# First distance bias: from ahead of the attention tiles into them, every second part by ScalarE and GpSimd

## The chip, the cores and the metric

The kernel runs on one core of a Trainium2 chip. The time is device microseconds of one launch. The core has TensorE (PE), VectorE (DVE), ScalarE (ACT), GpSimd (POOL) and SyncE (SP, which issues DMAs here). Each engine runs its own instructions in the order of the program and waits on semaphores for the others.

## The reference, cut to what matters

Four layers of cross-attention and feed-forward run over x (2 x 1024 tokens of 256). Only two things matter here. The first cross-attention adds no learned bias, only a mask:

```
logits = einsum('btnh,bfnh->bnft', k, q) + bias
weights = softmax(logits);  ctx = einsum('bnft,btnh->bfnh', weights, v)
```

The second cross-attention is a decoder of four layers, and each of these adds a bias made from a distance for each query and key (1024 x 77 for each of 2 batches), by a small net of 32 hidden units:

```
hbias = relu(dist[..., None] @ Wth + bth)     # 32 values for each distance
qs_bias = (hbias @ Wto + bto)[..., 0]
```

So the bias is bto plus mask plus 32 parts, and part j is Wto[j] * relu(Wth[j] * dist + bth[j]). The bias of the decoder's first layer needs nothing that the first attention computes. It is made during it.

## The kernel before

Tokens are handled in NT = 16 tiles of 128. A row of scores is 16 heads x 77 keys = 1232 wide. The first attention is stage n = 0 of `act_wide`, `dve_wide` and `pe_wide`. Ahead of its tiles the keys are folded into the query weights (L513, copied at L596 and L657) and the values multiplied by the output weights (`values`, ten times: PE L490, ACT copy L576). Between these PE makes six small products (L335) that DVE copies (L340). DVE also takes the statistics of x (L3892, L225), GpSimd makes the inverse root (L240 to L268), and DVE normalises the first two tiles (L278).

Then for each tile t:

- PE: scores of tile t+1 (L478), turns the normalised rows of tile t+2 (`turn_tile`, L407), turns the weights of tile t (L448, waits for DVE's `weights_made`), weighs the values (L456).
- DVE: adds the mask (L736), maximum (L708), shift (L710), then `after_shift()` with what is given to go between, then the sum (L713, waits for ACT's exponential), reciprocal (L715), weights (L717), and the residual of tile t-1 (L725, L727).
- ACT: normalises tile t+2 (L671), exponential of tile t (L581), `keep_tile(t + 2)` (L571, waits for PE's turned rows), three copies of the turned weights (L631), then `after(t)`.

The word hinge in the code is one part j of the bias. `act_first_hinge` (L1407) makes the relu into one of two buffers, `first_hinge[:, j % 2]`, and waits until part j-2 has been added, since it reuses that buffer. `dve_first_hinge` (L1421) multiplies by `wto` and adds to `first_bias` in one instruction, after the relu of part j and the addition of part j-1. The last part is written to `flat_bias`, the bias buffer of the tiles, free once the tiles' masks have been added.

ACT makes 16 relus ahead of the tiles and one at the end of each tile. DVE adds 15 parts ahead of the tiles, one in `after_shift()` of each of the 16 tiles, and the last one behind them (`first_event`). So the part that DVE adds in tile t is 15+t, and its relu was made in tile t-1 or earlier.

GpSimd, during the tiles, builds the six weight matrices of the quantised feed-forward (`pool_dequantise`, L1391, L1393, L1396, once DMAs have brought their scales) and an inverse root for the first six tiles, and is otherwise idle. `EARLY` is 3 pairs of tiles; `w_made` counts the matrices.

Of the kernel before, what the change touches and what calls it, by code (L numbers as in the profile page):

```python
# [11 lines left out]
ACT = mybir.ActivationFunctionType  # L12
# [6 lines left out]
NT = B * TB  # L19
# [5 lines left out]
NTE = HE // P  # L25
# [14 lines left out]
HINGES = 32  # L40
# [25 lines left out]
def build(nc, ctx, a, out):  # L66
# [496 lines left out]
    def act_wide(act, n, clears, late, tail, between, after):  # L563

        g0 = NT * n

        def keep_tile(t):
            act.wait_ge(turned, g0 + t + 1)
            if t >= 2:
                act.wait_ge(scored, g0 + t - 1)  # L570
            act.copy(xnTt[:, t % 2, :, :].rearrange("p k c -> p (k c)"), xt_bank(t)).then_inc(xt_kept, 1)  # L571

        def values(v):
            bt, c = v // (CH // 2), 2 * (v % (CH // 2))
# [24 lines left out]
        if late:  # L599
            for v in range(VT_USES):  # L600
                values(v)
                if between:
                    between(v)
            keep_tile(0)
            keep_tile(1)
            if between:
                between("rows kept")
        else:
            keep_tile(0)
            keep_tile(1)  # L610
            for v in range(3):
                values(v)
            power(0)
            for v in range(3, VT_USES):
                values(v)
        for t in range(NT):
            base = t % 2 * 3 * BANK
            if n == 0 and t + 2 < NT:
                act_normed(act, n, t + 2)
            if t or late:  # L620
                power(t)
            if t + 2 < NT:
                keep_tile(t + 2)
            if t == NT - 1 and tail:
                tail()
            if t >= 2:
                act.wait_ge(weighed, g0 + t - 1)
            for i, chunks in enumerate(WIDE_GROUPS):
                b0, m = chunks[0], len(chunks)
                act.wait_ge(p_turned, 3 * (g0 + t) + i + 1)  # L630
                act.copy(wide_probT[:, t % 2, b0:b0 + m, :].rearrange("p c n -> p (c n)"),  # L631
                         flat[:, base + b0 * P:base + (b0 + m) * P]).then_inc(p_kept, 1)
            if after:
                after(t)
# [595 lines left out]
    EARLY = 3  # L1230
# [134 lines left out]
                    vs()  # L1365

    def pool_quantised(pool):
        pool_root(pool, 1e-5, 0, 2 * EARLY)
        pool.wait_ge(rows_of_bias_landed, 16)
        for i in range(EVENTS + 1):  # L1370
            if i < EVENTS:
                pool.wait_ge(h_turned, i + 1)
                pool.tensor_tensor(pair_of(inner, i), pair_of(inner, i),
                                   brow[:, 2 * (i // PAIRS) + 1:2 * (i // PAIRS) + 2, :].to_broadcast([P, 2, D]), ALU.add).then_inc(h_biased, 1)
            if i >= 1:
                t = 2 * ((i - 1) % PAIRS)
                pool_root(pool, 1e-5, t, t + 2)
            if i == 1:
                pool_root(pool, 1e-5, 2 * EARLY, NT - 2)
                pool_root(pool, 1e-5, NT - 2, NT)  # L1380

    def pool_dequantise(pool):
        pool.wait_ge(quants_landed, 16 * 11)
        pool.wait_ge(products_kept, NL + KD)
        for j in range(NL):
            at = slice(j * KD * D, (j + 1) * KD * D)
            if j:
                pool.wait_ge(w_made, j)  # L1390
            pool.tensor_scalar(dequant, quants[:, at], 1.0 / 7.5, -1.0, ALU.mult, ALU.add).then_inc(pool_step, 1)  # L1391
            pool.wait_ge(pool_step, gs())
            pool.tensor_tensor(dequant, dequant, scales[:, KD * j:KD * j + KD, :].rearrange("p n o -> p (n o)"),  # L1393
                               ALU.mult).then_inc(pool_step, 1)
            pool.wait_ge(pool_step, gs())
            pool.tensor_tensor(WT[:, j, :, :].rearrange("p k o -> p (k o)"), WT[:, j, :, :].rearrange("p k o -> p (k o)"), dequant,  # L1396
                               ALU.add).then_inc(w_made, 1)

    def act_first_hinge(act, j):
        if j == 0:
            act.wait_ge(distance_landed, 64)
            act.wait_ge(fside_landed, 16)
        if j >= 2:
            act.wait_ge(hinge_added, j - 1)
        act.activation(first_hinge[:, j % 2, :], flat_side, ACT.Relu, scale=wth[:, j:j + 1], bias=bth[:, j:j + 1]).then_inc(hinge_made, 1)  # L1407

    def dve_first_hinge(dve, j):
        if j == 0:  # L1410
            dve.wait_ge(distance_landed, 64)
            dve.wait_ge(mask_landed, 16)
            by_tile = first_bias.rearrange("p (t s) -> p t s", s=S2)
            for bt in range(B):
                dve.tensor_scalar(by_tile[:, bt * TB:(bt + 1) * TB, :], mask[:, bt, :].unsqueeze(1).to_broadcast([P, TB, S2]),
                                  bto[:, 0:1], None, ALU.add).then_inc(dve_step, 1)
                dve.wait_ge(dve_step, vs())
        else:
            dve.wait_ge(hinge_added, j)
        dve.wait_ge(hinge_made, j + 1)  # L1420
        dve.scalar_tensor_tensor(first_bias if j < HINGES - 1 else flat_bias, first_hinge[:, j % 2, :], wto[:, j:j + 1], first_bias,  # L1421
                                 ALU.mult, ALU.add).then_inc(hinge_added, 1)


# [19 lines left out]
    class Hinges:  # L1444
# [15 lines left out]
        def dve(self, dve):  # L1460
# [6 lines left out]
                                      bto[:, 0:1], None, ALU.add).then_inc(dve_step, 1)  # L1467
                    dve.wait_ge(dve_step, vs())
            elif j < HINGES:
                dve.wait_ge(hinge_made, base + j + 1)  # L1470
                if j:
                    dve.wait_ge(hinge_added, base + j)
                dve.scalar_tensor_tensor(flat_bias, hinge[:, j % 2, :], wto[:, j:j + 1], flat_bias,  # L1473
                                         ALU.mult, ALU.add).then_inc(hinge_added, 1)
# [2391 lines left out]
    def act_program(act):  # L3866
# [1 line left out]
        hinges = iter(range(HINGES))  # L3868

        def between(done):  # L3870
            for _ in range({"values expanded": 2, "keys folded": 3, "rows kept": 4, 0: 0, VT_USES - 2: 0, VT_USES - 1: 0}.get(done, 1)):
                act_first_hinge(act, next(hinges))

        act_wide(act, 0, 1, True, lambda: act_quantised(act, 0, 2), between, lambda t: [act_first_hinge(act, j) for j in [next(hinges, None)] if j is not None])
        act.wait_ge(quants_landed, 16 * 11)
        act_quantised(act, 2, EVENTS + LAG_G)
        act_decoder(act)
# [4 lines left out]

    def dve_program(dve):
        dve_setup(dve)
        hinges = iter(range(HINGES))

        dve_wide_values(dve, 0, 1, lambda: dve_first_hinge(dve, next(hinges)))
        for _ in range(2):
            dve_first_hinge(dve, next(hinges))
        dve.wait_ge(x_landed, 48)  # L3890
        for t in range(NT):
            dve.bn_stats(bn6[:, t, :], x[:, t, :]).then_inc(dve_step, 1)  # L3892
            vs()
        dve_aggregate(dve)
        for j in range(2, NL):
            dve_first_hinge(dve, next(hinges))
            dve_first_hinge(dve, next(hinges))
            dve_lora(dve, j)
        dve_first_hinge(dve, next(hinges))
        dve.wait_ge(tanh_made, 1)  # L3900
        dve_root(dve)
        for t in range(2):
            dve_normed(dve, 0, x, t)
        for _ in range(3):
            dve_first_hinge(dve, next(hinges))

        def one_more(t):
            for j in [next(hinges, None)]:
# [10 lines left out]
        def first_event():  # L3919
            dve.wait_ge(rows_of_bias_landed, 16)  # L3920
            dve_quantised(dve, 0, 1)
            dve_aggregate(dve, 2 * EARLY, NT - 2)
            for j in hinges:
                dve_first_hinge(dve, j)

        dve_wide(dve, 0, x, tanh_g[:, 0:1], one_more, first_event)
        dve_aggregate(dve, NT - 2, NT)
# [7 lines left out]
    def pool_program(pool):  # L3935
# [3 lines left out]
        pool_centers(pool, 0, NT)  # L3939
        pool.wait_ge(products_kept, NL + KD)  # L3940
        pool_clear_pads(pool)
        pool_dequantise(pool)
        pool_quantised(pool)
        pool_clear_expanded(pool)
        pool.wait_ge(h_product, EVENTS)
# [71 lines left out]
```

## Time and profile before

| | us |
|---|---|
| median of 3 runs | 3079.68 (3072.37 to 3088.09) |
| the profiled execution | 3078.32 |
| its span | 3077.1 |
| before the first tile's mask addition | 65.0 |
| the 16 tiles of the first attention | about 65 to 224 |
| PE, DVE, ACT, POOL busy over the span | 96%, 68%, 40%, 28% |
| mean granted clock of TensorE | 0.989 |

Times in the rows are from the start of the span. A row of the timeline is one or several like instructions in order of time: start, how long, engine, line, what is written and read, how many, and in brackets how long the engine was idle before and which engine released it. The overall shares say little of this change, which lies in the first 230 us. There the stretches and the timelines tell.

### The profile page before, as it was taken

The page shows a single profiled execution, that of the slowest core. Times are in us where ns is not written, and L with a number is a line of the kernel's source. Part 1 is how long each engine was busy: PE and PEld are TensorE (multiplying, and loading weights), DVE is VectorE, ACT ScalarE, POOL GpSimd, SP SyncE. Part 2 cuts the span into 40 slices and gives each one's busy share as a digit, 9 for nine tenths or more (in the row PEclk, how much of TensorE's full clock was granted, in tenths as well). Part 3 has the DMA queues.
Part 4 walks back from the last instruction along what each step waited for, and adds up shares of the span by engine and source line. Part 5 has one row for each costly group of instructions (what it writes and reads, how often), then busy time and mean ns, then how long its engine had stood idle before and what let it go on. Part 6 is the DMA issues. An engine that isn't in the chain of part 4 may idle for free.

```text
span 3077.1 us, 44737 instructions
## 1 busy us (share of the span) xinstructions
PE 2951.9 (96%) x16886; PEld 2141.5 (70%) x16886; DVE 2089.9 (68%) x3855; ACT 1227.2 (40%) x2303; POOL 876.2 (28%) x1321
## 2 busy tenths in 40 slices
PE   7999899999999999999999999999999989998999
PEld 5778677667766776677689989866667754556565
DVE  6996689568856885687378898784317877774222
ACT  5443323553355335433233323451224556564232
POOL 2307300100110010001156565551342332111565
PEclk8999999999999999999999999999999999999999
DMA  7000100010002000200022222003361011113744
GB/s 186 28 1 1 58 1 1 14 44 28 1 14 72 1 1 14 71 1 1 1 85 82 89 82 83 30 1 110 130 246 56 4 46 53 33 47 131 212 85 98
DMA packets 106353, 172.32 MB, mean 56 GB/s; under 512 B 28842, under 2 KB 78925, under 8 KB 101405
## 3 DMA queue, kind: packets, MB, share of 16 engines
q1 hardware_dynamic: 87516, 98.10, 10.4%
q0 software_dynamic: 18624, 71.37, 7.6%
q8 instruction: 136, 2.23, 0.3%
q14 instruction: 77, 0.62, 0.1%
HBM read 193.86 MB, written 17.84 MB: 69 GB/s over the span
## 4 chain that ended last, share of the span: by engine, by line
PE 74%; DVE 15%; issue 4%; DMA 3%; ACT 3%; POOL 1%; SPq 0%; DVEq 0%; POOLq 0%; ACTq 0%
PE psum L456 8%; PE psum L478 8%; PE psum L1547 7%; PE psum L1559 7%; PE psum L2716 5%; PE psum L2028 5%; PE psum L1983 5%; PE psum L2737 3%; PE psum L1257 2%; PE psum L448 2%; PE psum L829 2%; PE psum L3368 2%; PE psum L2866 2%; DVE prep L1421 1%; PE psum L3388 1%
## 5 line engine op out<-in xcount | busy, mean ns | idle before, releaser
L456 PE MATMUL psum<-Vt,shared 128*128 128x256 f32 x1600 | 358.9, 379 | 0.2
L478 PE MATMUL psum<-Kt,xnTt 128*128 128x512 f32 (+1 forms) x960 | 348.6, 513 | 0.4 <-ACT xnTt L571 0.3
L456 PEld LDWEIGHTS psum<-Vt,shared 128*128 128x128 f32 x1600 | 297.7, 190 | 38.2 <-issue 1.0
L478 PEld LDWEIGHTS psum<-Kt,xnTt 128*128 128x128 f32 x960 | 181.0, 192 | 162.7 <-issue 159.1
L247 POOL TENSOR_SCALAR root_v<-meanvar 128x8 f32<-128x8 f32 (+3 forms) x19 | 8.6, 454 | 880.5 <-DVE meanvar L225 880.5
L1559 PEld LDWEIGHTS psum<-expert_w,prep 128*128 128x128 f32 x1024 | 194.6, 190 | 77.7 <-issue 57.4
L1559 PE MATMUL psum<-expert_w,prep 128*128 128x256 f32 x1024 | 240.8, 379 | 0.0
L1547 PE MATMUL psum<-weights,expert_w 128*128 128x512 f32 x512 | 240.3, 593 | 0.0
L1473 DVE SCALAR_TENSOR_TENSOR bias<-Kt,small,bias 128x1232 f32<-128x1232 f32 x96 | 149.2, 1554 | 129.3 <-ACT Kt L1457 128.4
L3657 DVE CUSTOM_DVE_ANT_0 psum<-psum,expert_w 128x128 f32<-128x128 f32 (+7 forms) x256 | 191.1, 777 | 65.9 <-PE psum L3368 61.9
L2823 DVE TENSOR_TENSOR prep<-psum,prep 128x512 f32<-128x512 f32 x62 | 42.9, 692 | 218.0 <-PE psum L2716 201.4
L3544 ACT ACTIVATE prep<-psum 128x512 f32<-128x512 f32 (+3 forms) x384 | 163.1, 504 | 63.6 <-PE psum L3391 61.5
L1602 ACT ACTIVATE prep<-psum,bias 128x512 f32<-128x512 f32 x128 | 87.9, 687 | 237.3 <-PE psum L1547 237.3
L581 ACT ACTIVATE shared<-shared 128x1232 f32<-128x1232 f32 x80 | 98.7, 1233 | 181.9 <-DVE shared L710 181.9
L713 DVE TENSOR_REDUCE row<-shared 128x16 f32<-128x1232 f32 x80 | 114.7, 1434 | 55.3 <-ACT shared L581 55.3
L571 ACT COPY xnTt<-psum 128x256 f32<-128x256 f32 x80 | 29.4, 372 | 298.9 <-PE psum L407 298.8
L1547 PEld LDWEIGHTS psum<-weights,expert_w 128*128 128x128 f32 x512 | 96.1, 190 | 69.1 <-issue 63.1
L736 DVE TENSOR_TENSOR shared<-psum,bias 128x1232 f32<-128x1232 f32 x80 | 115.0, 1438 | 36.5 <-PE psum L478 33.1
L1457 ACT ACTIVATE Kt<-fside,small 128x1232 f32<-128x1232 f32 x96 | 134.5, 1404 | 1.5 <-DVE bias L1473 1.5
L631 ACT COPY shared<-psum 128x512 f32<-128x512 f32 (+1 forms) x240 | 115.4, 517 | 39.7 <-PE psum L448 38.6
L3368 PE MATMUL psum<-weights 72*128 72x512 bf16 (+3 forms) x384 | 106.7, 333 | 19.7 <-DVE row L3657 18.0
L3388 PE MATMUL psum<-weights 75*128 75x512 bf16 (+3 forms) x384 | 113.0, 333 | 7.5 <-DVE Kt L3597 3.0
(529 smaller groups left out, 6546.5 us busy)
## 6 DMA issues: line engine op xcount, KB each, us to landing
weights<-in_L_ffn_w SPq DMA_DIRECT2D x32, 512.0 KB, 4.9
expert_w<-in_L_ffn_w SPq DMA_DIRECT2D x32, 512.0 KB, 4.8
expert_w<-in_L_xattn_Wf SPq DMA_DIRECT2D x16, 512.0 KB, 5.9
weights<-q_parts SPq DMA_DIRECT2D x31, 144.0 KB
weights<-k_parts SPq DMA_DIRECT2D x93, 48.0 KB
weights<-in_L_xattn_Wk SPq DMA_DIRECT2D x4, 1024.0 KB, 5.0
weights<-in_L_xattn_Wv SPq DMA_DIRECT2D x4, 1024.0 KB, 7.6
weights<-in_L_xattn_Wq SPq DMA_DIRECT2D x4, 1024.0 KB, 5.5
```

The lines of the kernel that those rows point to most:

```text
L456: ins = pe.matmul(o_bank(t), wide_probT[:, t % 2, c, :], Vt[:, t // TB, c, :], start=(c == 8), stop=(c == 7))
L478: ins = pe.matmul(flat[:, par * 3 * BANK + at:par * 3 * BANK + at + cols], xnTt[:, par, k, :], Kt[:, t // TB, k, src:src + cols], start=(k ...
L1473: dve.scalar_tensor_tensor(flat_bias, hinge[:, j % 2, :], wto[:, j:j + 1], flat_bias, ALU.mult, ALU.add).then_inc(hinge_added, 1)
L1547: ins = pe.matmul(bank, slot(s)[0][:, k, f * P:(f + 1) * P], xnT_of(g)[:, k, :], start=(k == 0), stop=(k == KD - 1))
L1559: ins = pe.matmul(y[:, t * D:(t + 1) * D], hidden[:, n % 4, t * P:(t + 1) * P], slot(s)[2][:, f, :], start=(n % GROUP_STEPS == 0 and t % 2 ...
L1983: return pe.matmul(product_of(i), lhs, rhs, start=start, stop=stop, skip_group_check=True)
L2028: ins = pe.matmul(acc_of(i)[:, t * P:(t + 1) * P], lhs[:, t * P:(t + 1) * P], rhs, start=(begin and start and t == 0), stop=end, skip_grou ...
L2716: ins = pe.matmul(psum[:, 2 * (c % 2) + n, :], rows_xT[:, c % 2, k, :], w[:, at:at + F], start=(k == 0), stop=(k == KD - 1))
L3368: ins = pe.matmul(flat[:, base + at:base + at + w], heads[0:STACK, 0, s, t * P:(t + 1) * P], heads[0:STACK, 1, s, at:at + w], start=True, ...
L3388: ins = pe.matmul(psum[:, bank, 0:w], heads[:, 1, s, j * P:(j + 1) * P], heads[:, 0, s, at:at + w], start=True, stop=True)
L3544: act.activation(expT[:, h % 2, to:to + w], psum[:, ring_bank(("piece", h, i)), 0:w], ACT.Exp, scale=float(HD3) ** -0.5).then_inc(exp_made, 1)
L3657: dve.tensor_tensor_reduce(flat[:, base:base + cols], flat[:, base:base + cols], later[:, S - cols:S], 1.0, -3.0e38, ALU.add, ALU.max, max ...
```

## The change

- The order of ACT: four relus ahead of the tiles (two behind the values' expansion, two behind the folded keys), none between the copies of the values. The other 28 are made two in each of tiles 0 to 13. For this `act_wide` calls `after(t)` a second time, behind `keep_tile(t + 2)` and ahead of the three copies.
- Odd parts from 5 on (14 parts) are not DVE's. ACT multiplies the relu by `wto` in place (a second instruction, which waits for the first) and GpSimd adds it to `first_bias`.
- DVE adds 18 parts: 0 to 3 ahead of the tiles, and 4, 6, ... 30 in `after_shift()` of tiles 0 to 13.
- GpSimd adds part 5+2j ahead of building matrix j, for six matrices, then two more, then the inverse root for the first six tiles, then six more; the last waits for all shifts and writes `flat_bias`.
- `hinge_made` now counts twice for an odd part, so the wait of the later layers has a constant more.

```diff
@@ act_wide, in the loop over tiles
             if t + 2 < NT:
                 keep_tile(t + 2)
+            if after:
+                after(t)
@@ pool_dequantise
         for j in range(NL):
+            pool_first_hinge(pool, next(hinges))
@@
+    HINGES_AHEAD = 4
+    def on_pool(j):
+        return j > HINGES_AHEAD and j % 2 == 1
+    def first_made_by(j):
+        return j + 1 + sum(map(on_pool, range(j + 1)))
+    def pool_first_hinge(pool, j):
+        pool.wait_ge(hinge_added, j)
+        if j == HINGES - 1:
+            pool.wait_ge(shifted, NT)
+        pool.wait_ge(hinge_made, first_made_by(j))
+        pool.tensor_tensor(first_bias if j < HINGES - 1 else flat_bias, first_hinge[:, 1, :], first_bias, ALU.add).then_inc(hinge_added, 1)
@@ act_first_hinge
-        act.activation(first_hinge[:, j % 2, :], flat_side, ACT.Relu, scale=wth[:, j:j + 1], bias=bth[:, j:j + 1]).then_inc(hinge_made, 1)
+        ins = act.activation(first_hinge[:, j % 2, :], flat_side, ACT.Relu, scale=wth[:, j:j + 1], bias=bth[:, j:j + 1])
+        if on_pool(j):
+            ins.then_inc(hinge_made, 1)
+            act.wait_ge(hinge_made, first_made_by(j) - 1)
+            ins = act.mul(first_hinge[:, 1, :], first_hinge[:, 1, :], wto[:, j:j + 1])
+        ins.then_inc(hinge_made, 1)
@@ dve_first_hinge
-        dve.wait_ge(hinge_made, j + 1)
+        dve.wait_ge(hinge_made, first_made_by(j))
@@ act_program
-            for _ in range({"values expanded": 2, "keys folded": 3, "rows kept": 4, 0: 0, VT_USES - 2: 0, VT_USES - 1: 0}.get(done, 1)):
+            for _ in range({"values expanded": 2, "keys folded": 2}.get(done, 0)):
@@ pool_program
-        pool_dequantise(pool)
+        hinges = iter(j for j in range(HINGES) if on_pool(j))
+        pool_dequantise(pool, hinges)
+        for _ in range(NTE - NL):
+            pool_first_hinge(pool, next(hinges))
+        pool_root(pool, 1e-5, 0, 2 * EARLY)
+        for j in hinges:
+            pool_first_hinge(pool, j)
```

Two places in the programs of the engines. First ACT, one tile near the start of the tiles, from the normalisation of tile t+2 (`xn`) to that of the next. `inner` is the hinge buffer. Before:

```order
L671 ACTIVATE xn<-x,center,rstd 128x256 [waits turned,factors_made]
L581 ACTIVATE shared<-shared 128x8x154 [waits shifted]
L571 COPY xnTt<-psum 128x256 [waits scored,turned]
L631 COPY shared<-psum 128x256 [waits p_turned]
L631 COPY shared<-psum 128x512 [waits p_turned] x2
L1407 ACTIVATE inner<-fside,small 128x1232 [waits hinge_added]
```

And now, the same place:

```order
L673 ACTIVATE xn<-x,center,rstd 128x256 [waits turned,factors_made]
L581 ACTIVATE shared<-shared 128x8x154 [waits shifted]
L571 COPY xnTt<-psum 128x256 [waits scored,turned]
L1426 ACTIVATE inner<-fside,small 128x1232 [waits hinge_added]
L633 COPY shared<-psum 128x256 [waits p_turned]
L633 COPY shared<-psum 128x512 [waits p_turned] x2
L1426 ACTIVATE inner<-fside,small 128x1232 [waits hinge_added]
L1430 ACTIVATE inner<-inner,small 128x1232 [waits hinge_made]
```

One relu has come between the exponential with the copy of the turned rows and the three copies. A multiplication has come behind the other relu. Second DVE, ahead of the tiles, from the statistics of x to the mask addition of tile 0. Before:

```order
L225 BN_AGGR meanvar<-bn6 128x2 x15
L1421 SCALAR_TENSOR_TENSOR prep<-inner,small,prep 128x1232 [waits hinge_made,hinge_added] x2
L340 COPY expert_w<-psum 128x512 [waits products_set_up]
...
L1421 SCALAR_TENSOR_TENSOR prep<-inner,small,prep 128x1232 [waits hinge_made,hinge_added]
L278 TENSOR_SCALAR xn<-x,meanvar,rstd 128x256 [waits root_made,tanh_made]
L278 TENSOR_SCALAR xn<-x,meanvar,rstd 128x256
L1421 SCALAR_TENSOR_TENSOR prep<-inner,small,prep 128x1232 [waits hinge_made,hinge_added] x3
L736 TENSOR_TENSOR shared<-psum,bias 128x8x154 [waits scored]
```

And now:

```order
L225 BN_AGGR meanvar<-bn6 128x2 x15
L340 COPY expert_w<-psum 128x512 [waits products_set_up] x4
L1445 SCALAR_TENSOR_TENSOR prep<-inner,small,prep 128x1232 [waits hinge_made,hinge_added]
L278 TENSOR_SCALAR xn<-x,meanvar,rstd 128x256 [waits root_made,tanh_made]
L278 TENSOR_SCALAR xn<-x,meanvar,rstd 128x256
L1445 SCALAR_TENSOR_TENSOR prep<-inner,small,prep 128x1232 [waits hinge_made,hinge_added]
L738 TENSOR_TENSOR shared<-psum,bias 128x8x154 [waits scored]
```

Of the twelve additions between the statistics and tile 0 two are left. Inside a tile DVE's own order is as it was: mask, maximum, shift, one part of the bias, sum.

## Rows read from the trace of the kernel before

**Rows 1.** Stretches: span, PE, PEld, DVE, ACT, POOL busy, clock, DMA, GB/s.

```profile
73.93:204.13 130.20, 128.02 (x572) 94.82 (x572) 127.99 (x128) 62.11 (x91) 26.90 (x22) 1.00 0.07 25
```

**Rows 2.** Waits from 66 to 222: who for whom, total us, times, longest.

```profile
ACT xnTt L571 <- PE psum L407: 49.9, 13, 4.4
```

**Rows 3.** Timeline of DVE: weights of tiles 0 and 13, and of a tile between.

```profile
72.46 1.46 DVE L717 TENSOR_TENSOR shared<-shared,row 128x1232 f32<-128x1232 f32 x1
...
139.12 1.49 DVE L1421 SCALAR_TENSOR_TENSOR prep<-inner,small,prep 128x1232 f32<-128x1232 f32 x1
...
142.28 1.44 DVE L717 TENSOR_TENSOR shared<-shared,row 128x1232 f32<-128x1232 f32 x1
...
202.69 1.44 DVE L717 TENSOR_TENSOR shared<-shared,row 128x1232 f32<-128x1232 f32 x1
```

**Rows 4.** Timeline of PE, one tile: turned weights, and the next scores.

```profile
84.06 1.31 PE L448 MATMUL psum<-ident,shared 128*128 128x128 f32 x10
...
89.53 4.30 PE L478 MATMUL psum<-Kt,xnTt 128*128 128x512 f32 x12
```

**Rows 5.** Timeline of ACT, the same tile.

```profile
84.54 1.51 ACT L631 COPY shared<-psum 128x256 f32<-128x256 f32 x3
85.93 1.43 ACT L1407 ACTIVATE inner<-fside,small 128x1232 f32<-128x1232 f32 x1
...
94.08 0.37 ACT L571 COPY xnTt<-psum 128x256 f32<-128x256 f32 x1 [2.96 <-PE psum L407]
```

**Rows 6.** Timeline, the last part: relu of ACT, then DVE, which waited.

```profile
225.94 1.43 ACT L1407 ACTIVATE inner<-fside,small 128x1232 f32<-128x1232 f32 x1
...
227.47 1.50 DVE L1421 SCALAR_TENSOR_TENSOR bias<-inner,small,prep 128x1232 f32<-128x1232 f32 x1 [0.41 <-ACT inner L1407]
```

**Rows 7.** Timeline, tile 0: DVE's mask addition, ACT's exponential and copy.

```profile
65.00 1.44 DVE L736 TENSOR_TENSOR shared<-psum,bias 128x1232 f32<-128x1232 f32 x1
...
69.42 1.23 ACT L581 ACTIVATE shared<-shared 128x1232 f32<-128x1232 f32 x1 [3.95 <-DVE shared L710]
70.56 0.35 ACT L571 COPY xnTt<-psum 128x256 f32<-128x256 f32 x1
```

**Rows 8.** Timeline ahead of the tiles: PE's values and products, GpSimd's root.

```profile
37.47 2.83 PE L490 MATMUL psum<-weights,prep 128*32 128x256 f32 x32 [2.53 <-ACT Vt L576]
40.23 2.07 PE L335 MATMUL psum<-shared 32*128 32x256 f32 x4
...
49.85 1.93 PE L490 MATMUL psum<-weights,prep 128*32 128x256 f32 x32
51.72 1.13 PE L335 MATMUL psum<-shared 32*128 32x256 f32 x4
...
49.15 1.34 POOL L268 TENSOR_TENSOR rstd<-rstd,root_w 128x16 f32<-128x16 f32 x1
```

**Rows 9.** Stretches: granted clock of TensorE ahead of the tiles.

```profile
46.00:48.00 2.00, 2.00 (x24) 0.67 (x20) 1.96 (x2) 2.00 (x3) 1.92 (x2) 0.50 0.00 0
```

**Rows 10.** Timeline of PE: the scores of tiles 0 and 1, in two attentions.

```profile
57.98 0.67 PE L407 MATMUL psum<-ident,xn 128*128 128x128 f32 x4 [2.69 <-DVE xn L278]
58.95 10.15 PE L478 MATMUL psum<-Kt,xnTt 128*128 128x512 f32 x24 [0.29 <-ACT xnTt L571]
...
378.02 11.04 PE L478 MATMUL psum<-Kt,xnTt 128*128 128x512 f32 x24
```

**Rows 11.** GpSimd: a wide addition by form, and one line with min/median/max in ns.

```profile
L1727 POOL TENSOR_TENSOR inner<-inner,small 128x1024 f32<-128x1024 f32 x16 | 41.6, 2603 | 186.3 <-DVE prep L278 173.8 <-DVE Kt L278 12.5
...
L1393 POOL TENSOR_TENSOR prep<-prep x6: 1267/1278/2335, 71.4 to 95.9; 128x512 f32<-128x512 f32 x6
```

**Rows 12.** Timeline: DVE beside GpSimd, DVE's extra rows, GpSimd at the end.

```profile
78.36 2.52 DVE L1421 SCALAR_TENSOR_TENSOR prep<-inner,small,prep 128x1232 f32<-128x1232 f32 x1
...
200.29 0.73 DVE L278 TENSOR_SCALAR inner<-x,meanvar,rstd 128x256 f32<-128x256 f32 x2
...
226.62 0.23 POOL L245 TENSOR_SCALAR root_v<-meanvar 128x2 f32<-128x2 f32 x1 [3.91 <-DVE meanvar L225]
```

More of the change, by code:

```diff
@@ L1367, in pool_quantised @@
     def pool_quantised(pool):
-        pool_root(pool, 1e-5, 0, 2 * EARLY)
         pool.wait_ge(rows_of_bias_landed, 16)
@@ L1380, in pool_quantised, with pool_dequantise @@
                 pool_root(pool, 1e-5, NT - 2, NT)
-    def pool_dequantise(pool):
+    def pool_dequantise(pool, hinges):
         pool.wait_ge(quants_landed, 16 * 11)
@@ L1419, in dve_first_hinge @@
             dve.wait_ge(hinge_added, j)
-        dve.wait_ge(hinge_made, j + 1)
-        dve.scalar_tensor_tensor(first_bias if j < HINGES - 1 else flat_bias, first_hinge[:, j % 2, :], wto[:, j:j + 1], first_bias,
+        dve.wait_ge(hinge_made, first_made_by(j))
+        dve.scalar_tensor_tensor(first_bias, first_hinge[:, j % 2, :], wto[:, j:j + 1], first_bias,
                                  ALU.mult, ALU.add).then_inc(hinge_added, 1)
@@ L1469, in dve @@
             elif j < HINGES:
-                dve.wait_ge(hinge_made, base + j + 1)
+                dve.wait_ge(hinge_made, base + j + 1 + first_made_by(HINGES - 1) - HINGES)
                 if j:
@@ L3870, in between, with beside @@
         def between(done):
-            for _ in range({"values expanded": 2, "keys folded": 3, "rows kept": 4, 0: 0, VT_USES - 2: 0, VT_USES - 1: 0}.get(done, 1)):
+            for _ in range({"values expanded": 2, "keys folded": 2}.get(done, 0)):
                 act_first_hinge(act, next(hinges))
-        act_wide(act, 0, 1, True, lambda: act_quantised(act, 0, 2), between, lambda t: [act_first_hinge(act, j) for j in [next(hinges, None)] if j is not None])
+        def beside(t):
+            for j in [next(hinges, None)]:
+                if j is not None:
+                    act_first_hinge(act, j)
+        act_wide(act, 0, 1, True, lambda: act_quantised(act, 0, 2), between, beside)
         act.wait_ge(quants_landed, 16 * 11)
@@ L3884, in dve_program @@
         dve_setup(dve)
-        hinges = iter(range(HINGES))
+        hinges = iter(j for j in range(HINGES) if not on_pool(j))
         dve_wide_values(dve, 0, 1, lambda: dve_first_hinge(dve, next(hinges)))
-        for _ in range(2):
-            dve_first_hinge(dve, next(hinges))
+        dve_first_hinge(dve, next(hinges))
         dve.wait_ge(x_landed, 48)
@@ L3895, in dve_program @@
         for j in range(2, NL):
-            dve_first_hinge(dve, next(hinges))
-            dve_first_hinge(dve, next(hinges))
             dve_lora(dve, j)
@@ L3903, in dve_program @@
             dve_normed(dve, 0, x, t)
-        for _ in range(3):
-            dve_first_hinge(dve, next(hinges))
+        dve_first_hinge(dve, next(hinges))
         def one_more(t):
@@ L3922, in first_event @@
             dve_aggregate(dve, 2 * EARLY, NT - 2)
-            for j in hinges:
-                dve_first_hinge(dve, j)
+            dve.wait_ge(hinge_added, HINGES)
         dve_wide(dve, 0, x, tanh_g[:, 0:1], one_more, first_event)
```

## The prediction

> **What bounds the kernel now.** I read the stretch of the first attention first, since the change lies in it. Between the weights of tile 0 and of tile 13 both PE (128.02 of 130.20) and DVE (127.99) are full [rows 1]. 13 tiles take 202.69 - 72.46 = 130.2 us, 10.0 each [rows 3]. ACT is half idle and GpSimd four fifths. So ACT's and GpSimd's busy time is free here, but not their place in the chain of waits. DVE's addition of one part (1.49 us) also is no loss in a tile: it stands between the shift and the sum, and the sum needs ACT's exponential (1.23) anyway [rows 3, 7].
>
> Next I read what ACT waits for inside a tile. Its copy of the turned rows, `keep_tile(t + 2)`, waited 49.9 us for PE in 13 of the tiles, 3.8 each [rows 2]. In PE's program the turn of tile t+2 stands behind the weighing of tile t-1 and the scores of tile t+1. One tile shows it: PE starts to turn the weights at 84.06, starts the next scores at 89.53 for 4.30, and only then turns the rows; ACT's copy runs from 94.08 to 94.45 [rows 4, 5]. From the moment the weights of a tile are there to the end of that copy is thus 94.45 - 84.06 = 10.39 us. Today nothing of DVE hangs on it within the tile.
>
> **The change, part by part.** *The new wait.* DVE adds part 4+2t in tile t, between shift and sum, and ACT makes the relu of just that part in the same tile, behind the exponential and behind `keep_tile(t + 2)`. Before, DVE's part was 15+t and its relu a tile old. Now DVE stands at the part until PE has turned the rows, ACT has copied them and made the relu. Queued behind it on DVE are the sum, the reciprocal and the weights, and PE waits for the weights to turn them, with the weighing and the next scores behind. That closes a loop through three engines, from weights to weights:
>
> - DVE to PE, a hand-over: 0.10 (the one from ACT to DVE is 227.47 - 227.37 = 0.10) [rows 6];
> - PE turns weights, weighs, scores, turns rows, ACT copies: 10.39 [rows 4, 5];
> - the relu: 1.43 less the 0.12 by which it starts ahead of the copy's end (85.93 against 86.05): 1.31 [rows 5];
> - ACT to DVE: 0.10 [rows 6];
> - DVE from part to the end of the weights: 142.28 + 1.44 - 139.12 = 4.60 [rows 3].
>
> The sum is 16.5 us. The steps between tiles 0 and 13 are 13, so 13 x 16.5 = 214.6 in place of 130.2: **+84.4**. The mask addition, maximum and shift of the next tile, ACT's exponential and the residual fit beside PE's 10.39 and cost nothing; that cover stays, since PE gets no less work. In tiles 11 to 13 two rows normalised between part and sum (0.65 each) were hidden partly and now lie in the loop: **+2.0** [rows 12]. For its 14 parts the turned rows exist in all tiles, 0 to 13 (t+2 below 16).
>
> *Tile 0.* From the mask addition to the exponential's start are 4.42 us, the copy ends at 5.91 [rows 7], then relu 1.31, 0.10 and DVE's 4.60: 11.9. Before, 65.00 to 73.92 = 8.9 [rows 3, 7]. **+3.0.**
>
> *The clock of TensorE.* In the loop PE works 10.4 us and stands about 6. The clock granted ahead of the tiles is 0.50, 1.2 GHz, in places [rows 9]. The scores of tiles 0 and 1 took 10.15 us with 2.69 us of idle time ahead of PE's turn before them, and 11.04 in the next attention; two tiles' scores at full clock take 2 x 4.30 = 8.60 [rows 4, 10]. So a stand that lets the clock fall costs 1.55 to 2.44 us. The lower bound is 0 (the clock holds), the upper 2.44. I take 1.55, the row with the shorter stand: 13 x 1.55 = **+20.2**.
>
> *Tiles 14 and 15* have no part. In tile 14 PE still has its weighing and scores of 9.77 (84.06 to 93.83) [rows 4] with the 1.55, 11.3 against about 9.7 now: **+1.7** (0 to 2).
>
> *Ahead of the tiles.* DVE loses 11 additions, 16.5 us of it, ACT 12 relus. That does not all come back. What is late next is either GpSimd's root, ready at 50.49 and 1.5 earlier if the statistics start one part earlier, which gives 49.0, rows normalised and turned until 50.7, scores of tile 0 (half of 10.15) until 55.8, and 9.2 us gained [rows 8, 10]. Or it is PE's values: from 37.47 less one relu, 36.0, eight values (four pairs of 1.93) and three products of 1.13 are 11.1 us at full clock; at the lower clock a product takes 2.07, 1.83 times as long, and all 20.3 [rows 8]. Bounds for the tiles' start are then 9.2 and 2.6 earlier. The clock was still low at 46 to 48 [rows 9]. With 12 us at that pace, 12 / 1.83 = 6.6 of the 11.1 are done at 48 and the other 4.5 at 52.5; 0.97 for turning and copying and 5.1 for the scores make 58.5 instead of 65.0: **-6.5**.
>
> *ACT's and GpSimd's new work.* The second relu and the multiplication (not in the trace; taken as another 1.4, bounds 1.2 and 1.5 from the exponential and the relu) begin behind the three copies, which end 1.99 us into the loop [rows 4, 5], so they end near 4.8. GpSimd's addition of 1232 elements: 2.60 x 1232/1024 = 3.1 us, up to 1.83 times that, 5.7, by the spread of its 512-wide one [rows 11]. It ends at 8 to 10.5, and DVE asks for it at 11.9. Its three instructions for a matrix follow and end before the next. So none of it is on the path: 0. It can lengthen a DVE instruction that runs beside it: 2.52 against 1.49 once [rows 12]. In the loop DVE stands while GpSimd adds, so I take 0, with 14 x 1.03 = 14.4 as the upper end. In the Trainium skill, "SBUF — State Buffer", section "Who interferes with whom", a DVE instruction with two SBUF inputs and a GpSimd instruction that reads SBUF block each other for the whole instruction, the later one waiting. By that rule the sum could be up to 14 x 3.1 = 43 us more, an estimate; the 2.52 agrees that there is such a cost, and the rule speaks against the change wherever DVE does not stand anyway.
>
> *The end.* DVE's last part (1.50) goes, but it stood ahead of a residual that waited for PE: 0. GpSimd's last part (3.1) fits the 3.91 us that it was idle there [rows 12]: 0, up to 2.
>
> Sum: -6.5 + 3.0 + 84.4 + 2.0 + 20.2 + 1.7 = +104.8. On the profiled execution's own 3078.3 this gives **3183.1**; it lies 1.4 below the median of the runs shown, which is less than they spread. The later layers keep their order.
>
> **The rivals.** (a) *The relu is early enough*, and the kernel gets faster: if DVE found the relu ready within about 1.3 us of its shift (the length of the exponential), the tiles would stay at 10.0 and only the start count: 3078.3 - 6.5 = 3072. For it speaks ACT's idle half; against it that ACT runs in order and the relu is third behind exponential and copy. 3 in 100.
>
> (b) *The wait without the loop*: if PE's turned rows were there when the exponential ends, as in tile 0, the stand would be 4.42 to 5.91 and the relu, 2.9 us a tile. 13 x 2.9 = 38, less 130.2 - 13 x 9.7 = 4 of old stalls, + 3.0 - 6.5 + 2.0: near 3111. Against it are the 3.8 us that ACT waits for PE in each tile [rows 2], with PE already full. 5 in 100.
>
> (c) *TensorE stays at 1.2 GHz* through the tiles: PE's 10 us of each tile get 1.83 times as long, +8.3, so 13 x 8.3 = 108 in place of 20.2: 3270. Against it are the scores of tiles 0 and 1, which took only 1.55 us more than at full clock, so that it came back within them [rows 10]. 4 in 100.
>
> **How the numbers follow.** The loop as worked out has 88 in 100. Its ends: -9.2 + 3.0 + 84.4 + 2.0 + 0 + 0 = +80 (3158) with the clock held, and -2.6 + 3.0 + 84.4 + 2.0 + 31.7 + 14.4 + 2 + 2 = +137 (3215). The range 3157 to 3213 leaves out the rivals and the far end. A measurement tells about 0.5%, 15 us. Faster by more: 3 in 100 at most, half of (a) being within 0.5%; I give 0.02, the same 0.02, slower 0.96.
>
> **What would show it.** In the trace after: DVE's part in a tile (L1445) with an idle time before it of some 6 us, released by ACT's relu; ACT's copy L571 waiting for PE, and the relu right behind it; PE's turned weights (L448) waiting for DVE in tiles 1 to 13; tiles 16 to 19 us apart, then under 12; the granted clock at 0.50 for a part of each tile; the first mask addition near 58.5. GpSimd's additions end before DVE asks. If the relu is ahead of the copy in time, or the tiles are under 13 us apart, the loop is wrong. If they are over 20, the clock or GpSimd was priced too low.

## The result, and the profile after

The changed kernel takes **3183.4 us** (median of 4 executions, 3180.6 to 3190.3) against 3078.5 (4 executions, 3072.4 to 3088.1): ratio **1.034** [1.032, 1.036], 104.9 us slower. The profiled execution is the slowest of the four, 3190.25 with a span of 3189.0, 111.9 above the span of before; terms read from it are some us larger than those of the median. The change acts up to the start of the scores of the second attention. Up to there the profiled execution takes 486.11 against 378.02 [rows 10], 108.1 more; the other 3.8 lie in the later layers, which the change leaves alone: from there to the end the twelve profiled executions of this document take between 2691 and 2707.

Stretches of the kernel after. The columns are those of [rows 1]; the first two lie ahead of the tiles, the next around the work of PE in tile 1, the last is nearly the whole of the tiles.

```profile
40.00:44.00 4.00, 4.00 (x57) 2.09 (x49) 2.53 (x14) 1.75 (x3) 3.16 (x2) 1.00 0.00 2
44.00:48.00 4.00, 3.26 (x39) 1.83 (x40) 2.94 (x5) 1.76 (x3) 1.56 (x9) 1.00 0.10 25
...
65.00:82.00 17.00, 12.74 (x44) 9.55 (x44) 6.52 (x5) 7.47 (x9) 5.92 (x4) 0.80 0.46 153
...
60.00:320.00 260.00, 168.21 (x605) 127.21 (x606) 138.12 (x139) 102.70 (x124) 58.58 (x37) 0.78 0.06 20
```

Where PE and DVE were both busy for 128 of 130 us [rows 1], they are now busy for 168 and 138 of 260, at a granted clock of 0.78. Nobody is the bound; everybody waits. Who waits for whom from 60 to 320 us:

```profile
POOL prep L1418 <- ACT inner L1430: 186.9, 13, 24.9
DVE prep L1445 <- ACT inner L1426: 120.3, 14, 10.4
PE psum L448 <- DVE shared L719: 92.0, 14, 7.1
...
ACT xnTt L571 <- PE psum L407: 64.5, 13, 5.6
```

Read the last three upwards: ACT's copy waits for PE's turned rows (49.9 before [rows 2]), DVE's part waits for the relu behind that copy, PE's turn of the weights waits for DVE. That is a ring. The first line is the longest and costs nothing, as run 3 shows: GpSimd is early. One turn of the ring, from the weights of tile 0 to those of tile 1, in the timelines of DVE, PE and ACT (start, us, engine, line, operation, in brackets the idle time before it and who ended it):

```profile
53.01 1.44 DVE L738 TENSOR_TENSOR shared<-psum,bias 128x1232 f32<-128x1232 f32 x1 [3.79 <-PE psum L478]
...
63.51 1.44 DVE L719 TENSOR_TENSOR shared<-shared,row 128x1232 f32<-128x1232 f32 x1
...
79.66 1.50 DVE L1445 SCALAR_TENSOR_TENSOR prep<-inner,small,prep 128x1232 f32<-128x1232 f32 x1 [10.41 <-ACT inner L1426]
...
82.83 1.44 DVE L719 TENSOR_TENSOR shared<-shared,row 128x1232 f32<-128x1232 f32 x1
...
309.18 1.44 DVE L719 TENSOR_TENSOR shared<-shared,row 128x1232 f32<-128x1232 f32 x1
...
319.28 1.44 DVE L719 TENSOR_TENSOR shared<-shared,row 128x1232 f32<-128x1232 f32 x1
...
323.34 1.44 DVE L738 TENSOR_TENSOR shared<-psum,bias 128x1232 f32<-128x1232 f32 x1 [1.77 <-PE psum L478]
...
330.79 2.41 DVE L719 TENSOR_TENSOR shared<-shared,row 128x1232 f32<-128x1232 f32 x1
```

```profile
65.10 2.37 PE L448 MATMUL psum<-ident,shared 128*128 128x128 f32 x10 [5.31 <-DVE shared L719]
67.26 6.22 PE L456 MATMUL psum<-Vt,shared 128*128 128x256 f32 x20
73.32 4.30 PE L478 MATMUL psum<-Kt,xnTt 128*128 128x512 f32 x12
...
84.33 2.40 PE L448 MATMUL psum<-ident,shared 128*128 128x128 f32 x10 [6.49 <-DVE shared L719]
86.52 5.14 PE L456 MATMUL psum<-Vt,shared 128*128 128x256 f32 x20
91.50 4.30 PE L478 MATMUL psum<-Kt,xnTt 128*128 128x512 f32 x12
```

```profile
77.88 0.37 ACT L571 COPY xnTt<-psum 128x256 f32<-128x256 f32 x1 [5.51 <-PE psum L407]
78.14 1.41 ACT L1426 ACTIVATE inner<-fside,small 128x1232 f32<-128x1232 f32 x1
...
96.05 0.37 ACT L571 COPY xnTt<-psum 128x256 f32<-128x256 f32 x1 [4.42 <-PE psum L407]
```

The relu ends at 79.55 and DVE starts at 79.66, after 10.41 us of standing; from there to the end of its weights are 84.27 - 79.66 = 4.61. PE, having stood for 5.31 or 6.49 us, is granted the lower clock when it starts: turning (1.31 at full clock [rows 4]) takes 2.4. From weights to weights it is 82.83 - 63.51 = 19.3, then 18.2, and so on in turns; turning and weighing take 8.22 (65.10 to 73.32) in one tile and 7.17 (84.33 to 91.50) in the next, against 5.47 before [rows 4].

### The profile page after: what moved, and what is told of

The parts are those of the page before. It is cut to its first block, busy times and chain, and to the rows that moved or that the text cites. A ratio compares the mean times of both kernels' runs of the same rounds, so it can differ in the third digit from the quotient of the medians.

```text
span 3189.0 us, 44752 instructions
## 1 busy us (share of the span) xinstructions
PE 2988.3 (94%) x16886; PEld 2171.8 (68%) x16886; DVE 2069.6 (65%) x3841; ACT 1247.1 (39%) x2317; POOL 901.4 (28%) x1335
## 4 chain that ended last, share of the span: by engine, by line
PE 76%; DVE 11%; issue 4%; ACT 3%; DMA 3%; POOL 2%; SPq 0%; DVEq 0%; POOLq 0%; ACTq 0%
PE psum L456 11%; PE psum L478 10%; PE psum L1571 7%; PE psum L1583 6%; PE psum L2052 5%; PE psum L2007 5%; PE psum L2740 4%; PE psum L448 3%; PE psum L1259 2%; PE psum L3392 2%; PE psum L831 2%; PE psum L2761 2%; DMA out<-shared,prep 2%; PE psum L2890 2%; PE psum L3412 2%
## 5 line engine op out<-in xcount | busy, mean ns | idle before, releaser
L456 PE MATMUL psum<-Vt,shared 128*128 128x256 f32 x1600 | 376.3, 392 | 0.2
L456 PEld LDWEIGHTS psum<-Vt,shared 128*128 128x128 f32 x1600 | 311.6, 199 | 43.1 <-issue 1.0
L448 PE MATMUL psum<-ident,shared 128*128 128x128 f32 x800 | 116.6, 300 | 98.2 <-DVE shared L719 98.2
L448 PEld LDWEIGHTS psum<-ident,shared 128*128 128x128 f32 x800 | 101.9, 155 | 105.4 <-DVE shared L719 96.2
L633 ACT COPY shared<-psum 128x512 f32<-128x512 f32 (+1 forms) x240 | 116.7, 517 | 125.3 <-PE psum L448 124.8
```

What stands on the lines that cost most here:

```text
L448: ins = pe.transpose(flat[:, base + c * P:base + (c + 1) * P], rows[:, c * P:(c + 1) * P], ident[:, :])
L456: ins = pe.matmul(o_bank(t), wide_probT[:, t % 2, c, :], Vt[:, t // TB, c, :], start=(c == 8), stop=(c == 7))
```

## The experiments

Ten runs, each with its own median, and a ratio to the kernel before, run beside it on the same chip. Runs 1 to 4 shared a chip, so did 5 to 7, and 9 and 10; the kernel before had medians of 3082.8, 3079.8, 3076.9 (run 8) and 3078.0 there, so medians of different chips compare only to some 6 us. Where it matters, the start of the second attention's scores in the profiled execution is given too.

### 1. Two more relus ahead: is it the wait?

```diff
-            for _ in range({"values expanded": 2, "keys folded": 2}.get(done, 0)):
+            for _ in range({"values expanded": 2, "keys folded": 2, "rows kept": 2}.get(done, 0)):
```

> The changed kernel with parts 4 and 5 made by ScalarE ahead of the tiles (behind the copies of the first two turned tiles), so that in tile t it makes 6+2t and 7+2t and VectorE's part 4+2t is a tile old. Theory (VectorE stands for a relu behind the copy of the turned rows, and that closes the loop): the stands go, tiles fall from 18.9 us to about 10, and the earlier start (12 us by the trace) is kept: 3066 to 3076. Rival (two parts a tile are too much beside the attention, for ScalarE or for GpSimd and VectorE together): tiles stay above 15, 3140 or more.

**3085.3**, ratio 1.0005 [0.999, 1.002], 9 above the upper end. ACT is now a part ahead, and 98 of the 105 us are gone: the wait is the cause. But the kernel isn't faster than before, although its first mask addition starts 12 us earlier. Its timelines of DVE, ACT and PE, one tile:

```profile
106.13 1.73 DVE L719 TENSOR_TENSOR shared<-shared,row 128x1232 f32<-128x1232 f32 x1
...
108.45 1.42 ACT L1426 ACTIVATE inner<-fside,small 128x1232 f32<-128x1232 f32 x1
...
109.76 1.33 ACT L633 COPY shared<-psum 128x256 f32<-128x256 f32 x3
...
110.27 4.56 PE L456 MATMUL psum<-Vt,shared 128*128 128x256 f32 x20 [1.03 <-ACT shared L633]
...
117.17 1.44 DVE L719 TENSOR_TENSOR shared<-shared,row 128x1232 f32<-128x1232 f32 x1
```

The relu stands ahead of the three copies of the turned weights, so PE waits 1.03 us to weigh in nine of the tiles, 9.3 in all, and such a tile takes 11.04 (117.17 - 106.13) instead of 10. The 13 steps from tile 0 to 13 take 147.7 in place of 130.2, which is more than that. Most of the rest are instructions of DVE that run long beside GpSimd: in tile 11 the two normalised rows take 3.21, in place of 0.73 [rows 12], beside an addition of 2.90, and the tile takes 12.8. Together they more than eat the 12 us of the start: the second attention's scores start at 382.9 against 378.0.

### 2. The odd relu before the copy of the rows

```diff
+            if after:
+                after(t)
             if t + 2 < NT:
                 keep_tile(t + 2)
-            if after:
-                after(t)
```

> The changed kernel with the first relu of a tile ahead of the copy of the turned rows instead of behind it; all else is the same, and VectorE still waits for a relu of its own tile. Theory: the stand shrinks to exponential plus relu, 2.7 us, TensorE is out of the loop, tiles of 12.3 to 12.8 us: 13 x 6.2 = 81 less than the changed kernel, 3100 to 3106. Rival (any wait for a relu of the same tile costs it, the copy does not matter): above 3150.

**3115.7**, ratio 1.011 [1.007, 1.014], 10 above the upper end; the tiles take 12.5 to 14.3. The relu doesn't wait for the copy any more, but a smaller ring takes its place, which I had not seen. Waits, and the timelines of GpSimd and DVE in one tile:

```profile
DVE prep L1445 <- POOL prep L1418: 41.9, 13, 4.5
```

```profile
113.04 2.81 POOL L1418 TENSOR_TENSOR prep<-inner,prep 128x1232 f32<-128x1232 f32 x1 [7.18 <-ACT inner L1430]
...
115.92 1.81 DVE L1445 SCALAR_TENSOR_TENSOR prep<-inner,small,prep 128x1232 f32<-128x1232 f32 x1 [3.61 <-POOL prep L1418]
```

The odd part now is the late one: its relu and multiplication stand behind the three copies, GpSimd adds only then, and DVE must wait for that sum before it adds its own part.

### 3. GpSimd's addition and ACT's multiplication one element wide

```diff
-        pool.tensor_tensor(first_bias if j < HINGES - 1 else flat_bias, first_hinge[:, 1, :], first_bias, ALU.add).then_inc(hinge_added, 1)
+        pool.tensor_tensor((first_bias if j < HINGES - 1 else flat_bias)[:, 0:1], first_hinge[:, 1, 0:1], first_bias[:, 0:1], ALU.add).then_inc(hinge_added, 1)
...
-            ins = act.mul(first_hinge[:, 1, :], first_hinge[:, 1, :], wto[:, j:j + 1])
+            ins = act.mul(first_hinge[:, 1, 0:1], first_hinge[:, 1, 0:1], wto[:, j:j + 1])
```

> The changed kernel with GpSimd's additions and ScalarE's multiplications one element wide instead of 1232, so 14 of the 32 parts are not added; the waits are the same. Theory: neither is on the path of the loop, 3178 to 3186, tiles still 18 to 19 us. Rival (GpSimd's 2.8 us additions or ScalarE's multiplication pace the tiles, or block VectorE): 36 us less or more, under 3150.

**3186.9**, ratio 1.033 [1.030, 1.037]: no gain, though 14 of the 32 parts are left out; the second attention's scores start at 485.3 against 486.1. In the changed kernel the new work of GpSimd and of ACT's multiplication costs nothing.

### 4. TensorE kept at work while it would stand

```diff
+            if n == 0 and 1 <= t <= 13:
+                pe.wait_ge(shifted, g0 + t + 1)
+                pe_stay_at_work(pe, flat[:, t % 2 * 3 * BANK:t % 2 * 3 * BANK + P], 26)
             pe_turn_wide(pe, n, t)
```

> The changed kernel with 26 idle matmuls of 128 columns on TensorE in the stand of each tile 1 to 13 (about 6.2 us, ending about when the weights come), into a score bank that is free by then. Theory (part of the loop is the clock that falls during the stand): granted clock 1.00 through the tiles, tiles of 16.6 to 16.9 us, 13 x 2.2 = 29 less than the changed kernel, 3150 to 3158. Rival (the clock costs nothing, the loop is longer for another reason): the same as the changed kernel, 3180 to 3187.

**3156.6**, ratio 1.024 [1.020, 1.027], 26.8 below the changed kernel, 30.3 below run 3 on the same chip, and 28.5 to the start of the second attention's scores. The edit fills 13 of the 14 stands: the one before PE turns tile 0's weights stays, and so the step from tile 0 to 1 still takes 19.5. The granted clock from 64 to 285 us is 0.98, and the loop can be seen bare in PE's timeline:

```profile
100.94 1.31 PE L448 MATMUL psum<-ident,shared 128*128 128x128 f32 x10 [0.68 <-DVE shared L722]
102.09 4.48 PE L456 MATMUL psum<-Vt,shared 128*128 128x256 f32 x20
106.41 4.30 PE L478 MATMUL psum<-Kt,xnTt 128*128 128x512 f32 x12
110.54 0.38 PE L407 MATMUL psum<-ident,xn 128*128 128x128 f32 x2
110.76 5.97 PE L413 MATMUL psum<-ident 128*128 128x128 f32 x52
117.41 1.31 PE L448 MATMUL psum<-ident,shared 128*128 128x128 f32 x10 [0.68 <-DVE shared L722]
```

117.41 - 100.94 = 16.47 us. The sum of the five steps was 16.5. In tiles 11 to 13 a step takes 17.12, 3 x 0.65 = 2.0 more in all, as predicted for the two normalised rows.

### 5. Where do the 12 us at the start go?

As run 1, with the additions and multiplications of run 3.

> The kernel with two more parts ahead (tiles of 11.0 us in the middle, no faster than before) and GpSimd's additions and ScalarE's multiplications one element wide, so 14 of the 32 parts are not added. Theory (in that kernel VectorE waits some 1.3 us a tile for an exponential that ScalarE's two relus and multiplication push back; without the 1.3 us multiplication most of that goes): tiles near 10, 3066 to 3074, 11 to 19 less than that kernel. Rival (what is left there is TensorE's own pace): within 5 us of it, 3080 to 3086.

**3073.4**, ratio 0.998 [0.997, 0.9995]. That lies in the theory's range, but by luck: the tiles still take 11.04 in the middle where it had 10, and `PE psum L456 <- ACT shared L633` still adds up to 12.4 us in 12 tiles. So the 1.0 us a tile is the relu's place ahead of the copies, as said under 1, and neither the multiplication nor GpSimd. What these two cost comes on top: 12 us by the medians of two chips, 6.0 by the start of the second attention's scores (376.99 against 382.94), and tiles 11 and 12 are back at 11.0.

### 6 and 7. The odd part in ACT's wait, the even one behind the copies

Run 6 has the order of run 2 and one relu more ahead (`"rows kept": 1`), so that the part that ACT makes before the copy of the rows is the odd one, and the one behind the copies the even one of the next tile. Run 7 has GpSimd's addition one element wide besides.

> The changed kernel with one more part ahead (part 4) and the first of a tile's two parts ahead of the copy of the turned rows, so that the relu and multiplication for GpSimd (2.8 us) fall into ScalarE's wait of 3.8 us for TensorE, and the relu for VectorE's next tile behind the three copies. Theory: no stand of VectorE, exponential and copies on time, tiles of 9.7 to 10, the earlier start kept: 3065 to 3073, faster than before. Rival (GpSimd's additions beside VectorE's two-operand instructions cost what the start gives): 3076 to 3084, no difference from before.

> The kernel with the odd parts ahead of the copy, GpSimd's additions one element wide (14 parts not added); ScalarE as there. The difference is what GpSimd's 2.8 us additions cost VectorE. Theory: 1 to 10 us less than that kernel. Rival: 15 us less or more.

Run 6: **3074.3**, ratio 0.998 [0.997, 0.9995] (12 executions). Run 7: **3058.8**, ratio 0.9935 [0.992, 0.995]. The theory had 1 to 10 us for the difference, the rival 15 or more. It is 15.4 by the medians and 11.8 by the start of the second attention's scores (375.52 against 363.73); no run shows where the other 3.6 come from. Either way GpSimd's 14 additions do cost something once DVE has no idle time. In run 7 most tiles take 9.67, and DVE is full. In the profiled execution of run 6, the slowest of its twelve, GpSimd, DVE and PE in one tile:

```profile
106.46 2.78 POOL L1418 TENSOR_TENSOR prep<-inner,prep 128x1232 f32<-128x1232 f32 x1 [2.94 <-ACT inner L1430]
106.48 4.05 DVE L719 TENSOR_TENSOR shared<-shared,row 128x1232 f32<-128x1232 f32 x1
...
110.59 2.40 PE L448 MATMUL psum<-ident,shared 128*128 128x128 f32 x10 [4.08 <-DVE shared L719]
```

DVE's product, started 0.02 after GpSimd's addition, takes 4.05 instead of 1.44, 2.61 more, nearly the 2.78 of GpSimd; PE stands for it and starts at the lower clock. The Trainium skill, "SBUF — State Buffer", section "Who interferes with whom", says that a DVE instruction with two SBUF inputs and a GpSimd instruction that reads SBUF block each other for the whole instruction; by that rule, the trace agrees. Such tiles are those in which GpSimd also builds its matrices: the steps from tile 0 to 6 take 11.7 more than in run 7 (up to 12.3 each), and the nine after them 0.2 more, although eight of the 14 additions lie there. They fall beside other instructions of DVE, which keep their length; GpSimd, then DVE:

```profile
131.62 3.13 POOL L1418 TENSOR_TENSOR prep<-inner,prep 128x1232 f32<-128x1232 f32 x1 [5.46 <-ACT inner L1430]
...
131.99 0.48 DVE L727 SCALAR_TENSOR_TENSOR x<-psum,tanh_g,x 128x256 f32<-128x256 f32 x1
132.50 0.43 DVE L729 BATCH_NORM_STATS2 bn<-x 128x6 f32<-128x256 f32 x1
132.93 1.44 DVE L738 TENSOR_TENSOR shared<-psum,bias 128x1232 f32<-128x1232 f32 x1
134.41 1.44 DVE L710 TENSOR_REDUCE row<-shared 128x16 f32<-128x1232 f32 x1
```

### 8 to 10. Placing GpSimd's work

All three start from run 6. In run 8 DVE makes the odd parts 5 to 13 itself, so that GpSimd has its matrices alone. Run 9 is run 8 in which each matrix, and each addition of GpSimd, waits until DVE has written the tile's weights. Run 10 is run 6 with that wait for the additions only.

```diff
     def pool_dequantise(pool, hinges):
...
         for j in range(NL):
-            pool_first_hinge(pool, next(hinges))
+            pool.wait_ge(weights_made, j + 1)
...
     def on_pool(j):
-        return j > HINGES_AHEAD and j % 2 == 1
+        return j > 13 and j % 2 == 1
...
     def pool_first_hinge(pool, j):
...
+        pool.wait_ge(weights_made, (j - 3) // 2)
...
         def one_more(t):
...
                     dve_first_hinge(dve, j)
+                    if j % 2 == 1:
+                        dve_first_hinge(dve, next(hinges))
```

> As the odd part ahead of the copies, but VectorE makes the odd parts 5, 7, 9, 11 and 13 itself, one more addition in each of tiles 1 to 5, and GpSimd adds only 15, 17, ... 31 (from tile 5 on), so that it has nothing but its matrices in the tiles before. All is computed. Theory (of the 15.4 us that GpSimd's additions cost, all arise in the tiles in which it also makes matrices, since from tile 6 on the tiles of that run took 9.67 to 9.77): the tiles 1 to 5 take 9.67 + 1.45 = 11.1 each, the rest 9.7; the time is that with GpSimd's additions one element wide and five VectorE additions, 3058.8 + 5 x 1.45 = 3066, 3062 to 3071. Rival (each addition of GpSimd costs the same wherever it stands, 15.4 / 14 = 1.1): 3066 + 9 x 1.1 = 3076, 3073 to 3080, with tiles of 10.8 from the sixth on.

> As the run before it (VectorE makes the odd parts 5 to 13, GpSimd adds from 15 on), and each of GpSimd's six matrices, and each of its additions, waits until VectorE has finished the tile's last product (L719), so that what GpSimd does falls beside VectorE's residual, the mask addition out of PSUM and the maximum. All is computed. Theory (in the run before, the six matrices in one row from 61.9 to 90.9 beside L712, the additions and L719 cost 5.1 in tiles 1 and 2, and one addition beside L719 cost 2.4): the tiles 1 to 5 come to 11.2 each, tile 5 loses the stretched L719; 3074.6 - 5.1 - 2.4 = 3067, 3063 to 3070. Rival (the row of matrices only shared in something else, the clock's fall, and the pacing moves it): 3072 to 3077.

> The odd part ahead of the copies with all 14 of GpSimd's additions, each of which waits until VectorE has finished the tile's last product (L719); the matrix follows it. All is computed. Theory (a collision with L719, 4.05 against 1.44 in one tile, makes the clock fall behind it): these go, but addition and matrix together are 2.8 + 3.2 = 6.0 long and VectorE gives only some 3.8 between L719 and the next L712, so that L712 and the addition behind it stay stretched by 1 to 2 a tile in tiles 1 to 5: 3058.8 + 5 x 1.5 = 3066, 3064 to 3071. Rival (the clock falls whatever stretches): 3071 to 3077, as without the wait.

Run 8: **3074.6**, ratio 0.999 [0.998, 1.0005], 3.6 above the theory's range and inside the rival's. But the rival needed tiles of 10.8 from the sixth on, and from tile 6 on they take 9.7 to 10.3, as in run 7. With no part in between, GpSimd made its six matrices in one row from 61.9 to 90.9, beside DVE's shift and additions, and from mask addition to mask addition tiles 1 and 2 took 12.9 and 13.8. I had not thought of what paced them: the parts did. Run 9: **3071.8**, ratio 0.998 [0.997, 0.999]; run 10: **3073.1**, ratio 0.998 [0.997, 0.9996]. Both are some 2 above their expected ends, at or inside the ranges of their rivals, which had the clock as the cause. The traces speak against these: in tiles 1 to 5 of both PE turns the weights in 1.31, at full clock. In run 9 nothing is stretched in tiles 1 to 5; weights of DVE and the start of a matrix on GpSimd:

```profile
71.44 1.44 DVE L719 TENSOR_TENSOR shared<-shared,row 128x1232 f32<-128x1232 f32 x1
...
82.65 1.44 DVE L719 TENSOR_TENSOR shared<-shared,row 128x1232 f32<-128x1232 f32 x1
```

```profile
72.98 0.62 POOL L1393 TENSOR_SCALAR prep<-expert_w 128x512 f32<-128x512 int32 x1 [7.45 <-DVE shared L719]
...
75.03 1.28 POOL L1398 TENSOR_TENSOR expert_w<-expert_w,prep 128x512 f32<-128x512 f32 x1
```

Such a tile takes 11.2, DVE's 9.67 and one addition more. But the wait places the first addition of GpSimd behind the sixth matrix, and so beside DVE's shift in the next tile, which takes 12.0 in place of 9.7:

```profile
121.08 2.79 POOL L1419 TENSOR_TENSOR prep<-inner,prep 128x1232 f32<-128x1232 f32 x1
...
121.41 3.76 DVE L712 TENSOR_TENSOR shared<-shared,row 128x1232 f32<-128x1232 f32 x1
```

In run 10 the product keeps its 1.44 from tile 2 on, and the shift and DVE's part are stretched by 1.0 each beside the matrix, so that the four steps from tile 2 to 6 take 11.7, as its theory had it:

```profile
86.88 2.49 DVE L712 TENSOR_TENSOR shared<-shared,row 128x1232 f32<-128x1232 f32 x1
89.29 2.51 DVE L1446 SCALAR_TENSOR_TENSOR prep<-inner,small,prep 128x1232 f32<-128x1232 f32 x1
```

The second attention's scores start at 376.6 in run 8, 372.9 in run 9 and 373.4 in run 10, against 375.5 in run 6, 363.7 in run 7 and 378.0 before. Runs 6, 9 and 10 are all faster than the kernel before, by 0.2%, and can't be told from each other by their medians. What they keep of run 7's gain is small: either DVE pays for five additions (5 x 1.5 = 7.5) or it is stretched as long (2.1 a tile). Run 9 has the lowest median here of the versions that compute everything, 6 us under the kernel before, which is less than the spread of single executions.

## Why the prediction was right, point by point

The total was predicted as 3183.1 and is 3183.4; that close, it is luck in part: two errors of opposite sign, and an execution-to-execution spread of 10 us. By the terms, in the profiled execution, the slowest of four (starts of DVE's weights and mask additions; L719 of after answers to L717 in [rows 3]):

| term | predicted | measured |
|---|---|---|
| start of the first mask addition | -6.5 | 53.01 - 65.00 = -12.0 |
| tile 0 | +3.0 | 10.50 - 7.46 = +3.0 |
| 13 steps from tile 0 to 13 | +106.6 | 245.67 - 130.23 = +115.4 |
| tile 14 | +1.7 | 10.10 - 9.67 = +0.4 |
| tile 15 | 0 | 11.51 - 9.66 = +1.9 |
| from there to the second attention's scores | 0 | 155.32 - 156.00 = -0.7 |
| sum | +104.8 | 486.11 - 378.02 = +108.1 |
| later layers | 0 | 111.9 - 108.1 = +3.8 |

- **The loop** was right in its ring and in its size. The waits are the named ones, run 1 takes them away and the time goes with them, and run 4 shows 16.47 us where 16.5 were summed from rows of the kernel before.
- **The clock** had the right mechanism and too small a price. 13 x 1.55 and 1.7 for tile 14 made 21.9; run 4 gives 26.8 by the medians and 28.5 by the traces, of which 26.2 lie between tiles 0 and 13, 2.2 in each of the 12 steps whose stand it fills, and 2.3 in tiles 14 and 15. In the profiled execution the copy of the rows ends 78.25 - 65.10 = 13.15 and 96.42 - 84.33 = 12.09 after PE's start against the summed 10.39, so 2.76 and 1.70 in turns, 2.2 on average. I had taken the row with the shorter stand (2.69 us [rows 10]); the stand of the row that gave 2.44 was 11.03. The stands here, 5.3 and 6.5, lie between the two, and so does their average cost. The length of one stand alone doesn't tell the clock: run 8 has a stand of 3.59 us after which PE turned in 1.31, and run 6 one of 2.75 after which it took 2.22. Tile 14's share arrives in tile 15, where the mask addition waits 1.77 for PE's scores.
- **The start** was mis-sized, beyond its bound of 9.2. The failed step is "the clock was still low at 46 to 48": the stretch that was at 0.50 [rows 9] is at 1.00 in the kernel after. PE's waits there were ACT's copies of the values, queued behind relus (2.53 us [rows 8]); with the relus gone PE stands for 0.99 us at most there, and the clock does not fall; this is read from the two traces, no run isolates it. Both bounds kept a part of the old pace. GpSimd's root too was read at its old pace. Its first power takes 2.94 us after and 4.13 before, when DVE's additions ran beside it, and its last product (L268) 0.22 in place of 1.34 [rows 8], so that the root is ready at 45.24, 5.2 earlier and not 1.5:

```profile
41.12 2.94 POOL L260 TENSOR_TENSOR rstd<-root_v,minus_half 128x16 f32<-128x16 f32 x1
...
45.02 0.22 POOL L268 TENSOR_TENSOR rstd<-rstd,root_w 128x16 f32<-128x16 f32 x1
```

With the root out of the way and PE at full clock, the prediction's own steps on PE give 36.0 + 11.1 + 0.97 + 5.1 = 53.2; the trace has 53.01.

- **GpSimd at 0** was right for this kernel (run 3). The reason was right too, that DVE stands while GpSimd adds: where it doesn't, the same additions cost 11.8 to 15.4 (runs 6 and 7). That is near the 14 x 1.03 = 14.4 kept as the upper end, but not as 1.0 each: nearly all of it arises in the six tiles with matrices, and the eight additions behind them cost 0.2 together. So it is also far from the 43 that every addition blocking DVE for its whole length would make: most fall beside instructions of DVE that they don't stretch.
- **Rivals.** Rival (a), an early relu, needed an order of ACT that the changed kernel doesn't have; run 6 has it and comes to 3074 (the rival had 3072). Rival (b) had 3111; run 2, which opens the loop and leaves a stand, came to 3115.7, by another wait, so that the nearness is chance. (c) did not occur: PE's scores run at full clock, 4.30, in every tile.

## What to carry to other kernels

An engine that is half idle still runs in order: before work is put into it, ask what stands ahead of it in its queue and what that waits for. Here one relu, 1.4 us of free time, placed behind a copy that waits for TensorE, made a ring through three engines at 16.5 us in place of a 10 us tile; the place just in front of that copy, with the parts one step ahead, costs nothing (run 7). A ring is priced by adding its rows once around, and a stand of TensorE in it costs again through the clock.

## What was not expected of the hardware

- A TensorE stand of 5 to 7 us a tile cost 2.2 us a tile by itself, through the granted clock, and 52 idle 128-wide matmuls in each of 13 stands (5.97 us) gave 26.8 us back.
- Taking relus from ACT far ahead of TensorE's work went with a start 12.0 us earlier, more than either old pace had allowed: the granted clock at 40 to 48 us went from 0.50 to 1.00.
- A collision of GpSimd and VectorE can be paid more than once: 2.6 us in the 4.05 us product, and again in PE's turn at the lower clock (2.40 instead of 1.31) and its weighing. How the 11.8 us between runs 6 and 7 split between the two was not measured.
- The same addition of GpSimd stretched DVE's product by 2.6 us (run 6) or its shift by 2.3 (run 9) when they fell together, and left DVE's residual, mask addition and maximum as long as they were.
